# The last two batches of a gated cross-attention and mixture-of-experts kernel: new instruction orders, batch 6's down projections in another PSUM bank, and two of batch 7's four products with routing weights on VectorE

## What is computed

```python
x = x + tanh(g_xattn[0]) * xattn(layernorm(x), ctx_512, ...)
xf = layernorm(x)
combine = route(xf, router_weight, router_bias)   # (tokens, 16), four non-zero weights each
for e in range(16):
    g, u = xf @ w_gate[e].T, xf @ w_up[e].T
    out = out + combine[:, e:e + 1] * (silu(g) * u @ w_down[e].T)
x = x + tanh(g_ffn[0]) * out
```

## Time and profile before

| | us |
|---|---|
| median of 3 runs | 349.12 (349.02 to 356.06) |
| the profiled execution | 349.41 |
| its span, first to last instruction | 347.6 |
| PE busy in it | 318.1 |
| DVE busy | 256.4 |
| ACT busy | 196.2 |
| POOL busy | 151.1 |

### The profile page before, as it was taken

The page is one execution under the profiler, slowest core; times in us unless marked ns, Lnnn a source line. Parts: engine busy times, 40 slices in busy tenths (PEclk is TensorE's granted clock), DMA queues, the critical chain, the costliest instruction groups (busy, mean ns, idle before and its releaser), DMA issues.

```text
span 347.6 us, 8679 instructions
## 1 busy us (share of the span) xinstructions
PE 318.1 (92%) x3186; PEld 247.7 (71%) x3186; DVE 256.4 (74%) x639; ACT 196.2 (56%) x399; POOL 151.1 (43%) x176
## 2 busy tenths in 40 slices
PE   1579599989999999999999999999999999978696
PEld 0455365666687788778887888787888787856665
DVE  4238666868898888988798888888889854748742
ACT  2433356767667765687637765675666467532041
POOL 3884061404470588047633494318410722903422
PEclk9856759999999999999999999999999999989999
DMA  4269674688563855537655365077156005214000
GB/s 123 68 183 188 146 194 115 145 209 187 199 151 103 184 131 149 143 96 151 147 139 133 88 172 140 20 152 183 34 124 141 0 18 90 37 50 88 16 1 15
DMA packets 32889, 40.45 MB, mean 116 GB/s; under 512 B 3440, under 2 KB 29824, under 8 KB 30368
## 3 DMA queue, kind: packets, MB, share of 16 engines
q1 hardware_dynamic: 32004, 38.46, 46.7%
q10 hardware_dynamic: 844, 1.45, 1.7%
HBM read 29.84 MB, written 7.45 MB: 107 GB/s over the span
## 4 chain that ended last, share of the span: by engine, by line
PE 76%; DVE 7%; DMA 6%; SPq 5%; POOL 2%; issue 2%; ACT 1%; POOLq 0%; DVEq 0%
PE bank L918 15%; PE bank L846 14%; PE bank L825 8%; PE bank L943 7%; PE bank L800 7%; PE bank L803 6%; PE bank L822 5%; DMA k_stack<-tri_k 4%; SPq L427 2%; PE bank L893 2%; DVE row_max L1011 2%; PE bank L861 2%; PE bank L852 2%; SPq L426 1%; PE bank L956 1%
## 5 line engine op out<-in xcount | busy, mean ns | idle before, releaser
L1011 DVE TENSOR_REDUCE row_max<-bank 128x2 f32<-128x512 f32 (+1 forms) x224 | 146.9, 686 | 43.0 <-PE bank L803 24.9
L709 ACT ACTIVATE probs<-bank 128x512 f32<-128x512 f32 x224 | 127.5, 595 | 57.5 <-PE bank L825 27.7
L918 PE MATMUL bank<-xn2T,w_pairs_sb 128*128 128x256 f32 x256 | 68.0, 392 | 1.5 <-issue 0.9
L846 PE MATMUL bank<-probs,v_ext 128*32 128x256 f32 (+1 forms) x1024 | 57.2, 365 | 0.0
L626 POOL TENSOR_TENSOR f_h<-f_h,comb 128x512 f32<-128x512 f32 x32 | 40.3, 1273 | 36.1 <-DMA comb<-c_scr 20.4
L803 PE MATMUL bank<-k_stack,q_stack 72*128 72x256 bf16 x256 | 49.9, 284 | 2.7 <-DVE row_max L1011 2.1
L918 PEld LDWEIGHTS bank<-xn2T,w_pairs_sb 128*128 128x128 f32 x256 | 44.7, 193 | 8.3 <-issue 2.8
L825 PE MATMUL bank<-q_stack,k_stack 73*128 73x256 bf16 x256 | 49.2, 284 | 1.0 <-DMA q_stack<-shiftT 0.9
L412 POOL TENSOR_TENSOR rest<-proj,part 128x512 f32<-128x512 f32 x14 | 16.2, 1160 | 74.7 <-ACT part L682 74.6
L846 PEld LDWEIGHTS bank<-probs,v_ext 128*32 128x32 f32 x1024 | 30.0, 112 | 19.9 <-issue 4.7
L800 PE MATMUL bank<-k_stack,q_stack 121*128 121x128 bf16 (+1 forms) x384 | 39.1, 231 | 2.4 <-DMA k_stack<-tri_k 1.9
(11 more groups left out here) (113 smaller groups left out, 367.9 us busy)
## 6 DMA issues: line engine op xcount, KB each, us to landing
k_stack<-k_scr SPq DMA_DIRECT2D x45, 192.0 KB
q_stack<-q_scr SPq DMA_DIRECT2D x14, 576.0 KB
comb<-c_scr SPq DMA_DIRECT2D x14, 512.0 KB, 6.7
q_scr<-part SPq DMA_DIRECT2D x46, 64.0 KB
k_scr<-part SPq DMA_DIRECT2D x46, 64.0 KB
x_in<-in_x SPq DMA_DIRECT2D x8, 128.0 KB, 2.4
w_pairs_sb<-in_w_pairs SPq DMA_DIRECT2D x1, 1024.0 KB, 7.8
out<-y_out SPq DMA_DIRECT2D x8, 128.0 KB, 1.9
```

Of the source, the lines that this page charges most:

```text
L709: nc.scalar.activation(probs[:, seq % NP, :], exp_bank[s % 2][:, :], ACT.Exp).then_inc(exp_done, 1)
L846: last = pe.matmul(pv_bank[32 * n:32 * n + VW, col + q0:col + T], v[:, VW // 2 * odd:VW // 2 * odd + VW], weights, start=odd == 0 and kt = ...
L918: last = pe.matmul(bank_of[:, n * T:(n + 1) * T], w[:, e0:e0 + 128], xn2T[:, :], start=True, stop=True)
L1011: nc.vector.tensor_reduce(row_max[:, kind, qt, h0:h0 + nh], max_bank[k % 2][:, :].rearrange("p (h k) -> p h k", h=nh), AX.X, ALU.max).then ...
```

## The change

Four edits. (1) In the orders, batch 6's `combT`, which stood in front of `pv:7:3`, goes behind `wp:7`; `y:7:1` and `yT:7` go each one expert step forward; ACT and DVE follow (`yT_e:7` and `combT_e:6` before `tanh:6:1`; `m:7:1` before `swish:6`; `x1:7` and `stats2:7` before `swish:6:1`). (2) `ga:7` goes before `down:6`, and `up:7` between `down:6:4` and `down:6:5`, so `combT:7` stands directly behind `down:6:7`. (3) For batch 6 the down projections go to `pv_bank`, and `ga:7` waits no more for `out:6`. (4) In batch 7, the products with routing weights of rounds 1 and 3 are made by DVE (`lhc`), those of rounds 0 and 2 by POOL. SP's order is not changed.

```diff
@@ ORDERS 'pe'
-        combT:6 pv:7:3 ga:6 up:6 y:7:1 ga:6:1 yT:7 up:6:1 wp:7 ga:6:2 up:6:2 ga:6:3 up:6:3 xn2T:7 logits:7 down:6
-        down:6:1 down:6:2 down:6:3 down:6:4 down:6:5 down:6:6 down:6:7 ga:7 combT:7 up:7 sprd:7 ga:7:1 up:7:1 sprd:7:1
+        pv:7:3 ga:6 y:7:1 up:6 yT:7
+        ga:6:1 wp:7 combT:6 up:6:1 ga:6:2 up:6:2 ga:6:3 up:6:3 xn2T:7 logits:7 ga:7 down:6
+        down:6:1 down:6:2 down:6:3 down:6:4 up:7 down:6:5 down:6:6 down:6:7 combT:7 sprd:7 ga:7:1 up:7:1 sprd:7:1
@@ ORDERS 'act'
-        rt:6 exp_e:7:22 exp_e:7:23 exp_e:7:24 exp_e:7:25 exp_e:7:26 exp_e:7:27 combT_e:6 pv_e:7:1 tanh:6 tanh:6:1
-        yT_e:7 tanh:6:2 tanh:6:3 xn2T_e:7 rt:7 tanh:7 combT_e:7 tanh:7:1 sprd_e:7 sprd_e:7:1 tanh:7:2 sprd_e:7:2
+        rt:6 exp_e:7:22 exp_e:7:23 exp_e:7:24 exp_e:7:25 exp_e:7:26 exp_e:7:27 pv_e:7:1 tanh:6 yT_e:7 combT_e:6 tanh:6:1 tanh:6:2 tanh:6:3 xn2T_e:7 rt:7 tanh:7 combT_e:7 tanh:7:1 sprd_e:7 sprd_e:7:1 tanh:7:2 sprd_e:7:2
@@ ORDERS 'dve'
-        tup:5:3 route:6 route:6:1 route:6:2 route:6:3 m:7 route:6:4 route:6:5 out:5 swish:6 m:7:1 tup:6 swish:6:1
-        tup:6:1 x1:7 stats2:7 swish:6:2 tup:6:2 xnv2:7 swish:6:3 tup:6:3 route:7 route:7:1 route:7:2 route:7:3 out:6
-        route:7:4 route:7:5 swish:7 tup:7 swish:7:1 tup:7:1 swish:7:2 tup:7:2 swish:7:3 tup:7:3 out:7''',
+        tup:5:3 route:6 route:6:1 route:6:2 route:6:3 m:7 route:6:4 route:6:5 out:5 m:7:1 swish:6 tup:6 x1:7 stats2:7 swish:6:1 tup:6:1 swish:6:2 tup:6:2 xnv2:7 swish:6:3 tup:6:3 route:7 route:7:1 route:7:2 route:7:3 out:6
+        route:7:4 route:7:5 swish:7 tup:7 swish:7:1 tup:7:1 lhc:7:1 swish:7:2 tup:7:2 swish:7:3 tup:7:3 lhc:7:3 out:7''',
@@ ORDERS 'pool'
-        fhc:6:2 fhc:6:3 fhc:7 fhc:7:1 fhc:7:2 fhc:7:3''',
+        fhc:6:2 fhc:6:3 fhc:7 fhc:7:2''',
@@ build
+        last_hc_done = sem("last_hc_done")
+        def down_bank(b):
+
+            return pv_bank if b == B - 2 else gate_bank
@@ gates_of, j == 0
-                    ge(pe, out_made, b)
+                    ge(pe, out_made, b if b < B - 1 else 0)
@@ down
                 if j == 0:
                     pe.wait_ge(f_gate_done, b * GP + GP)
-                pe.wait_ge(f_hc_done, b * GP + j // 2 + 1)
+                    if b == B - 2:
+                        pe.wait_ge(pv_copied, 2 * B)
+                if b == B - 1 and j // 2 % 2 == 1:
+                    pe.wait_ge(last_hc_done, j // 4 + 1)
+                else:
+                    pe.wait_ge(f_hc_done, b * GP + (j // 4 if b == B - 1 else j // 2) + 1)
                 for n in range(NQ):
-                    last = pe.matmul(gate_bank[:, n * 128:(n + 1) * 128], f_h[:, j, n * 128:(n + 1) * 128], w_down[:, j, :],
+                    last = pe.matmul(down_bank(b)[:, n * 128:(n + 1) * 128], f_h[:, j, n * 128:(n + 1) * 128], w_down[:, j, :],
@@ vector
+            def combine_last(b, j):
+                dve.wait_ge(ups_free, b * GP + j + 1)
+                dve.wait_ge(spread_done, j + 1)
+                at = f_h[:, 2 * j:2 * j + 2, :]
+                nc.vector.tensor_tensor(at, at, comb[:, 2 * j:2 * j + 2, :], ALU.mult).then_inc(last_hc_done, 1)
+                elif what == "lhc":
+                    combine_last(b, n)
@@ out
-                    nc.vector.tensor_tensor(y_out[:, :, :], gate_bank[:, 0:T].rearrange("p (n c) -> p n c", n=NQ),
+                    nc.vector.tensor_tensor(y_out[:, :, :], down_bank(b)[:, 0:T].rearrange("p (n c) -> p n c", n=NQ),
```

## The result

The change made the kernel slower. The median after it is 355.55 us (353.23 to 360.07, 4 runs), against 351.17 (349.02 to 356.06, 4 runs) for the kernel before timed beside it; the ratio is 1.0145, 95% interval 1.0086 to 1.0203. The forecast was 351.2, a loss of 1.8 us, with a range of 348.0 to 354.0. The profiled execution took 353.86 us, with a span of 352.1. (In a few executions a kernel is some per cent slower for no reason of its own; the ratios leave these out, while the medians hold them.)

What follows compares the result with a forecast made beforehand. PE was taken as the bound (busy 92% of the span), with 13.77 us of unbroken PE work from sprd:7:0; its start, 332.95 against 331.13, gave 349.41 + 1.82 = 351.2 us, range 348.0 to 354.0.

Steps and rivals of the forecast that it cites:

- Attention's end: End of batch 7's attention: comes forward by 4 us, with yT:7 at 311.5 instead of 315.65 and x1 from 313.3.
- combT:6 late: Batch 6's routing weights: combT:6 goes back by 6 us, its copy ready at 314.7 instead of 308.75.
- The landing: Load of batch 6's routing weights: 7.8 us from first cin issue at 316.15, so POOL starts fhc:6 at 323.95.
- rival 2: Weights land within 6.0 us of cin:6, so fhc:6 is no obstacle; 1.2 us faster, 348.2 us; chance 0.13.
- PE and the routing behind it: From down:6 to sprd:7:0: PE waits for POOL's products, held routing costs nothing, sprd:7:0 at 332.95, 1.8 us late.
- The bank edit: Around down:6: removes the 0.91 us stop and lifts out ga:7 and up:7 (1.8 us), all turning into waiting for products.
- The products on DVE: Batch 7's two products moved from POOL to DVE: priced at 0 (bounds 0 and +0.4 us), covered by PE's work.
- The clock: PE's clock falling behind new standstills near down:6: left out of the sum, a rival giving 352.3 to 354.0, chance 0.32.
- rival 1: Clock falls on top: about 1.1 us in down:6, 1.7 us behind 332; 352.3 to 354.0 us, chance 0.32.
- The level it was counted from: Base of the sum: the profiled execution of the kernel before, 349.41 us, taken as 0.29 above the runs' median.

Runs made afterwards that it cites:

- the run with the wait filled: Changed kernel plus five unused matmuls on PE between ga:7 and down:6, while POOL waits for the weights; profiled execution 351.91 us, tail 39.07 us.
- the bank edit's run: Kernel before with only down:6 in the values' bank, ga:7 ahead of down:6 and up:7 between down:6:4 and down:6:5; profiled execution 352.00 us.
- The changed kernel's second profile: The changed kernel, unchanged, timed in more rounds and profiled once more; 356.17 us, ratio 1.0168 to the kernel before.
- the run with both waits filled: Changed kernel plus unused PE matmuls, five between ga:7 and down:6 and three between down:6:7 and combT:7; 355.11 us, ratio 1.0063 to the kernel before.
- out:6 behind the routing: Changed kernel with combT:6 before ga:6, out:6 after batch 7's routing and swish:7 on DVE, combT:7 before down:6:7; 347.45 us, ratio 0.9949 to the kernel before.
- the run with the weights early: Changed kernel with combT:6 put back in front of ga:6 and combT_e:6 before tanh:6 on ACT; profiled execution 354.85 us, tail 39.30 us.
- 128 rows in the kernel before: Kernel before with only batch 7's spreading matmuls over 128 array rows instead of 16; 350.00 us, ratio 0.9961.
- the one with 128 rows: Version with out:6 behind the routing, plus batch 7's spreading matmuls over 128 array rows instead of 16; 346.93 us, ratio 0.9871 to the kernel before.

## Why the prediction was wrong

The mechanism and the step times were right, and the size of the loss was not: the falls of the clock behind the new standstills were left out of the sum, and the level from which it was counted was that of one favourable execution. Step by step:

- **Attention's end.** yT:7 was expected at 311.5 with out:5 at 307.73, 3.8 behind it; it came at 313.00 - 309.07 = 3.93. x1: 5.6 expected, 5.72 measured. Right.
- **combT:6 late.** The copy was to end at 314.7, 7.0 behind out:5; it ended at 316.12, 7.05. Right.
- **The landing.** From the first issue to fhc:6 7.8 us were taken and 325.27 - 317.59 = 7.68 measured; fhc:6 was due 16.2 behind out:5 and came at +16.20. Right, though the 7.8 was picked between bounds of 7.1 and 9.05; in the ten profiles in which POOL waited for this load it was 7.67 to 7.98 us. The estimate of 4.5 us from the Trainium skill (DMA: Bandwidth & Descriptors, Anatomy of one DMA), whose fit is for DMAs issued from POOL, doesn't agree: it is some 3 us too short for these two loads, and rival 2, which rested on such a landing, fails with it.
- **PE and the routing behind it.** In the run with the wait filled, with no fall of the clock, sprd:7:0 came at +25.19; my sum was 332.95 - 307.73 = 25.22. The bank edit turned into waiting, as forecast. DVE instructions were held by POOL one at a time (L1065 1.05 us instead of 0.17, L1071 1.28 for two instead of 0.26), and that cost nothing.
- **The products on DVE**: priced at 0, measured 0. They took 0.69 us each, not 0.93.
- **The clock: here the prediction failed.** The sum has no term for it. The kernel before showed a fall behind a standstill of 1.9 us, and my own sum had a standstill of 2.4 us; still I made the fall a rival with a chance of 0.32. All three profiles of this order without fillers have one, from 328.3, 328.7 and 326.4 us on, behind or at the end of standstills of 2.44, 2.56 and 2.65 us, and it cost 1.26 us where the filled wait measures it (1.1 in rival 1). Two of the three have a second fall behind sprd:7:0, at a cost of 1.64 us (1.7 in rival 1). So the prices were right, and the chance too low. It was no certainty either: the bank edit's run has a standstill of 2.33 us without a fall. Rival 1 with both falls ends at 354.0, and with the measured prices at 351.2 + 1.26 + 1.64 = 354.1; the falls of the tail alone don't reach the measured median of 355.55.
- **The level it was counted from.** The sum stood on one execution, whose out:5 started at 307.73. The same head took up to 3.4 us longer in other profiles, the four latest with a fall near 78 us. The runs shown, 349.02 to 356.06, said so, and the range took no account of it. Without head and fall the profiled execution gives the forecast: 353.86 - 1.34 - 1.26 = 351.26. The changed kernel's second profile adds up in the same way: 349.41 + 3.24 (head) + 4.59 (tail) = 357.24 us.

What stays open: why the tail's +3.1 to +4.6 us come with ratios that stand for +5.1 and +5.9 us (the intervals reach down to 3.0 and 3.6; falls in the head of some executions would explain it, but only one execution of each run has a trace), and where the two groups of times in the run with both waits filled lose their time.

## What to carry to other kernels

When a step that feeds a long DMA is moved behind others, count the whole way back, copy, issue, store, load and landing, and compare it with the moment at which its user is ready: here the 6.0 us by which the copy came later used up 2.2 us of cover and put the first product back by 3.9 us. An edit that lifts work out of a stretch is worth nothing if this work was what covered a chain on another engine; look at what was hidden beneath it, and move that chain too (out:6 behind the routing). A new standstill on PE has to be priced twice, once for itself and once for a likely fall of the clock: of the eight standstills of 1.9 to 5.4 us in the tails of these profiles, seven came with one.

## What the runs showed of the hardware

- **Matmuls of 16 rows among matmuls of 128 rows cost PE time beyond their own.** From sprd:7:0 to the last y_out it was 13.87 or 13.88 us with 16 rows (the six profiles with no fall in this stretch) and 12.50 or 12.51 us with 128 rows (three profiles), for the same number of matmuls. PE goes seven times from the one height to the other there; if the whole difference is put down to these changes, which was not tested by itself, a change costs an estimated 1.36 / 7 = 0.19 us.
- **The clock can fall while PE is busy throughout.** In the run with the weights early (stretches of 1 us, as above):

```profile
343.00:344.00 1.00, 1.00 (x5) 0.61 (x4) 0.31 (x1) 0.60 (x1) 1.00 (x1) 1.00 0.00 0
344.00:345.00 1.00, 1.00 (x4) 0.82 (x4) 0.37 (x1) 0.60 (x1) 0.00 (x0) 0.62 0.00 0
345.00:346.00 1.00, 1.00 (x5) 0.82 (x4) 0.00 (x0) 0.00 (x0) 0.00 (x0) 0.50 0.00 0
```

  PE had been busy without a break since 333.2, and at the full clock since 337.6, when it fell again at 344.2. Falls behind sprd:7:0 came in five of eleven profiles with spreads of 16 rows and in none of three with 128 rows. Those at 331 to 339 stand close behind a standstill of 1.42 us at r_w in four of the five, but the same standstill had no fall behind it in two other profiles (changed, one wait filled); those at 341 and 344, and that at 339 in the version with out:6 behind the routing, do not. That the height of the matmuls is their cause fits this, but three profiles don't show it.
- **One order has its fall in some executions and not in others.** The kernel before had the one at 309 in both profiles; the bank edit's kernel, whose order is the same up to there, had none, behind a standstill of 2.33 us against 1.91 and 2.34, and was 1.63 us earlier at xnv2:7. With 128 rows in the kernel before, the one at 310 came, and another at 327, which neither profile of the kernel before has. Nor does it take a long standstill: the falls near 322, in the version with out:6 behind the routing and in the one with 128 rows, had no stop longer than about 1.0 us in the 4 us before them.
- **Two loads of 512 KB each, spread over the partitions,** took 7.67 to 7.98 us from the first issue until POOL, which waited for them, could start (ten profiles).
